# A token's residual row travels with its gathered row, and the scatter writes whole rows (fused graph layer and mixture of experts, one Trainium2 core)

## What is computed

```
xn = layernorm(x)
x  = x + gnn(xn, src, dst, edge_weight) + mix(xn)      # graph sum, linear attention, two small layers
h  = layernorm(x)                                      # "h2" in the kernel
expert = argmax(h @ gate_w + gate_b) ; prb = its softmax value ; pos = rank of the token in its expert
kept   = pos < C                                       # C = ceil(1.25 * 12500 / 8)
y  = (relu(h @ w1[expert] + b1[expert]) @ w2[expert] + b2[expert]) * prb * kept
x  = x + nan_to_num(y, nan=0, posinf=1e4, neginf=-1e4)
```

## Time and profile before

| | |
|---|---|
| three plain runs | 2583.5, 2587.7, 2589.4 us; median 2587.7 us |
| the profiled execution | 2590.2 us, of which the trace spans 2588.4 us |
| PE | 2050 us busy, 79% |
| POOL | 1887 us, 73% |
| PE weight loads | 1593 us, 62% |
| DVE | 1465 us, 57% |
| ACT | 1022 us, 39% |
| DRAM traffic | 503 MB read, 75 MB written, mean 223 GB/s |
| granted TensorE clock, mean | 0.91 of full speed |

### The profile page before, as it was taken

How to read it: one execution, slowest core, us unless ns; L and a number is a source line. 1 busy time by engine, 2 the same in 40 slices (tenths; PEclk the granted TensorE clock), 3 DMA queues, 4 the chain that set the end, 5 groups by cost and what they waited for, 6 DMA issues and landing times. The chain is left out here.

```text
span 2588.4 us, 42537 instructions
## 1 busy us (share of the span) xinstructions
PE 2050.1 (79%) x12806; PEld 1592.5 (62%) x12806; DVE 1464.9 (57%) x5075; ACT 1021.6 (39%) x2450; POOL 1887.3 (73%) x1891
## 2 busy tenths in 40 slices
PE   0079999964677778998889889678888889877687
PEld 0035665543465557777777777557677777676677
DVE  6765555543567777776456456456656656554122
ACT  4643333321444445543343443334443434442233
POOL 7377777777777777777777777777777777736675
PEclk9999999986888889999999999888998989897899
DMA  9755666544566676766776776656887888788997
GB/s 338 258 163 166 174 172 170 167 136 140 171 177 181 176 246 201 220 222 214 229 236 211 231 240 182 214 187 239 297 280 263 268 284 273 262 260 234 295 320 241
DMA packets 294748, 578.36 MB, mean 223 GB/s; under 512 B 51837, under 2 KB 208109, under 8 KB 272271
## 3 DMA queue, kind: packets, MB, share of 16 engines
q1 hardware_dynamic: 164097, 294.27, 33.5%
q0 software_dynamic: 100032, 242.92, 32.7%
q10 hardware_dynamic: 30390, 38.41, 4.1%
HBM read 503.32 MB, written 74.92 MB: 223 GB/s over the span
## 5 line engine op out<-in xcount | busy, mean ns | idle before, releaser
L826 POOL DMA_INDIRECT rows_sb<-xn_scratch,src_sb x1600 | 1549.5, 968 | 526.1 <-issue 519.8
L907 PE MATMUL bank<-rows_sb,s_sb 128*24 128x256 f32 x3200 | 247.9, 433 | 267.3 <-DMA rows_sb<-xn_scratch,src_sb 261.3
L1094 PE MATMUL bank<-acc 128*128 128x256 f32 x1680 | 423.6, 398 | 41.1 <-DVE acc L1583 13.5
L1075 PE MATMUL bank<-acc 128*128 128x128 f32 (+1 forms) x2624 | 437.3, 323 | 15.8 <-issue 15.1
L1075 PEld LDWEIGHTS bank<-acc 128*128 128x128 f32 x2624 | 389.4, 207 | 40.3 <-issue 17.2
L1817 ACT ACTIVATE acc<-bank,acc 128x128 f32<-128x128 f32 (+1 forms) x656 | 212.1, 397 | 452.5 <-PE bank L1075 445.9
L1094 PEld LDWEIGHTS bank<-acc 128*128 128x128 f32 x1680 | 327.2, 202 | 87.2 <-issue 39.5
L1350 DVE TENSOR_TENSOR acc<-acc,bank 128x48 f32 x832 | 170.4, 205 | 293.0 <-PE bank L917 188.9
L907 PEld LDWEIGHTS bank<-rows_sb,s_sb 128*24 128x24 f32 x3200 | 91.5, 110 | 347.9 <-issue 318.9
L1742 ACT COPY sums<-bank 120x256 f32<-120x256 f32 x208 | 76.5, 368 | 395.8 <-PE bank L907 394.2
L1773 ACT ACT_TABLE_LOAD x95 | 121.9, 1283 | 174.7 <-PE bank L996 173.8
(11 more groups left out here) (228 smaller groups left out, 3442.1 us busy)
## 6 DMA issues: line engine op xcount, KB each, us to landing
acc<-ffn_first_in SPq DMA_DIRECT2D x82, 1028.0 KB
acc<-ffn_w_in SPq DMA_DIRECT2D x82, 1024.0 KB
rows_sb<-xn_scratch,src_sb POOLq DMA_INDIRECT x1600
arena<-xn_scratch SPq DMA_DIRECT2D x194, 128.0 KB, 3.1
xnt_scratch<-arena SPq DMA_DIRECT2D x97, 128.0 KB, 2.0
arena<-xnt_scratch SPq DMA_DIRECT2D x97, 128.0 KB
arena<-x_in SPq DMA_DIRECT2D x97, 128.0 KB
h_scratch<-arena ACTq DMA_DIRECT2D x97, 128.0 KB
```

The source lines that it names most:

```text
L826: pool.indirect_dma_start(out=rows_sb[:, c % ROW_SLOTS, :], out_offset=None, in_=xn_d, in_offset=bass.IndirectOffsetOnAxis(ap=src_sb[:, c: ...
L907: m = pe.matmul(psum[0][i * COLS:i * COLS + WIN, 0:D], s_sb[:, p % S_SLOTS, i * GROUP + j, :], early_row(c) if p < EARLY_PAIRS else rows_s ...
L1075: m = pe.matmul(bank[:, i * tokens:(i + 1) * tokens], w1_sb[k % 2][:, h, f * P:(f + 1) * P], xt[:, k % 2, h, 0:tokens], start=h == 0, stop ...
L1094: m = pe.matmul(bank[:, i * D:(i + 1) * D], hid[:, f, i * P:(i + 1) * P], w2_sb[k % 2][:, f, :], start=f == 0 and i == 0, stop=f == FC - 1 ...
```

## The change

- `h2_d` has rows of 2 KB: the layernorm and, behind it, `x` itself. ACT stores both with one DMA (and `out` as before).
- The gather of a unit brings both halves into a ring of eight token tiles, `tok` (2 KB per row). The result is computed in place over the first half, DVE adds the second half to it as the last of its operations, and the scatters, direct and kept, write whole rows without `compute_op`.
- As `tok` is also the place of the result, a gather waits on POOL until the unit that held its tiles before has been stored (`kept_st`) or scattered (`y_st`). DVE's waits for these ahead of L1583 go away.
- DVE cleans tile by tile (the buffers for mask and clipped value are one tile wide).
- The kept units 0 to 20, which SP stored three places behind their last tick's place (`done_place`), are stored one place behind it. All other places stay.

```diff
-    ACC_W = max(WIDE_WINDOWS * WIDE, T * P, N + WIN)
+    ACC_W = max(WIDE_WINDOWS * WIDE, T * P, N + WIN) + 100
+    TOKENS = 8
...
-        h2_d = nc.dram_tensor("h2_scratch", [N, D], F32).ap()
+        h2_d = nc.dram_tensor("h2_scratch", [N, 2 * D], F32).ap()
...
-        xs = behind(1, 2 * UNIT_TILES, D)
+        tok = behind(1, TOKENS, 2 * D)
...
-        yo = behind(1, YS * UNIT_TILES, D)
-        mask_sb = behind(1, UNIT_TILES, D)
-        clip_sb = behind(1, UNIT_TILES, D)
+        mask_sb = behind(1, D)
+        clip_sb = behind(1, D)
...
+        def token_slots(k):
+            at = units[k][1] % TOKENS
+            assert at + size(k) <= TOKENS
+            return slice(at, at + size(k))
+
+        def held_before(k):
+            taken_by = {i for i in range(k) if set(columns_of(i)) & {c - TOKENS for c in columns_of(k)}}
+            return sorted(taken_by)
...
-            lag = 3 if done_place(k) < PAIRS - 3 and size(min(k + 2, K - 1)) == UNIT_TILES else 1
-            scatter_at[min(done_place(k) + lag, PLACES - 1)].append(k)
+            scatter_at[min(done_place(k) + 1, PLACES - 1)].append(k)
...
                 at = col % BACK_ROWS * D
+                if k >= YS:
+                    sp.wait_ge(kept_st[k % YS], kept_value(k - YS))
                 sp.wait_ge(y_done, k + 1)
-                sp.dma_start(kept_d[col // BACK_ROWS, :, at:at + n * D],
-                             yo[:, k % YS * UNIT_TILES:k % YS * UNIT_TILES + n, :].rearrange("p i d -> p (i d)")
-                             ).then_inc(kept_st[k % YS], 16)
+                sp.dma_start(kept_d[col // BACK_ROWS, :, at:at + n * D].rearrange("p (i d) -> p i d", i=n),
+                             tok[:, token_slots(k), 0:D]).then_inc(kept_st[k % YS], 16)
...
                 if k >= 2:
                     pool.wait_ge(x_turned, k - 1)
-                for i, col in enumerate(columns_of(k)):
+                for i in held_before(k):
+                    if i < len(kept):
+                        pool.wait_ge(kept_st[i % YS], kept_value(i))
+                    else:
+                        pool.wait_ge(y_st[i % YS], y_value(i))
+                for col in columns_of(k):
                     pool.indirect_dma_start(
-                        out=xs[:, k % 2 * UNIT_TILES + i, :], out_offset=None, in_=h2_d[0:tokens, :],
+                        out=tok[:, col % TOKENS, :], out_offset=None, in_=h2_d[0:tokens, :],
...
             def scatter_unit(k):
                 tokens = min((routes[batch_of[k]][-1] + 1) * P, N)
+                if k - YS >= len(kept):
+                    pool.wait_ge(y_st[k % YS], y_value(k - YS))
                 pool.wait_ge(y_done, k + 1)
-                for i, col in enumerate(columns_of(k)):
+                for col in columns_of(k):
                     pool.indirect_dma_start(
                         out=out[0:tokens, :], out_offset=bass.IndirectOffsetOnAxis(ap=sca_i[:, col:col + 1], axis=0),
-                        in_=yo[:, k % YS * UNIT_TILES + i, :], in_offset=None, bounds_check=tokens - 1, oob_is_err=False,
-                        compute_op=ALU.add).then_inc(y_st[k % YS], 16)
+                        in_=tok[:, col % TOKENS, 0:D], in_offset=None, bounds_check=tokens - 1, oob_is_err=False
+                    ).then_inc(y_st[k % YS], 16)
...
                     in_=rows_sb[:, s * BACK_ROWS + col % BACK_ROWS, :], in_offset=None,
-                    bounds_check=tokens - 1, oob_is_err=False, compute_op=ALU.add).then_inc(back_st[s], 16)
+                    bounds_check=tokens - 1, oob_is_err=False).then_inc(back_st[s], 16)
...
-                        if k >= YS and k - YS < len(kept):
-                            dve.wait_ge(kept_st[k % YS], kept_value(k - YS))
-                        elif k >= YS:
-                            dve.wait_ge(y_st[k % YS], y_value(k - YS))
...
-                        link(dve.tensor_tensor(mask, y, y, ALU.not_equal))
-                        link(dve.copy_predicated(y, mask, nil[:, :].unsqueeze(2).broadcast_to([P, size(k), D])))
+                        for i in range(size(k)):
+                            link(dve.tensor_tensor(mask, y[:, i, :], y[:, i, :], ALU.not_equal))
+                            link(dve.copy_predicated(y[:, i, :], mask, nil[:, :].broadcast_to([P, D])))
                     elif step == FLUSH:
-                        link(dve.tensor_scalar(clip, y, 10000.0, -10000.0, ALU.min, ALU.max))
-                        link(dve.tensor_scalar(mask, y, 0.0, 0.0, ALU.mult, ALU.not_equal))
-                        dve.copy_predicated(y, mask, clip).then_inc(y_done, 1)
+                        for i in range(size(k)):
+                            link(dve.tensor_scalar(clip, y[:, i, :], 10000.0, -10000.0, ALU.min, ALU.max))
+                            link(dve.tensor_scalar(mask, y[:, i, :], 0.0, 0.0, ALU.mult, ALU.not_equal))
+                            link(dve.copy_predicated(y[:, i, :], mask, clip))
+                        dve.tensor_tensor(y, y, kept_row, ALU.add).then_inc(y_done, 1)
...
-                    act.dma_start(h2_d[t * P:t * P + r, :], c_out[0:r, t % OS, 0, :]).then_inc(c_st[t % OS], 16)
+                    act.dma_start(h2_d[t * P:t * P + r, :], flat2(c_out[0:r, t % OS, :, :])).then_inc(c_st[t % OS], 16)
```

More of the change, by code:

```diff
@@ L252, in build @@
         b2_sb = [behind(1, D) for _ in range(2)]
-        xs = behind(1, 2 * UNIT_TILES, D)
+        tok = behind(1, TOKENS, 2 * D)
         xt = behind(1, 2, H, UNIT)
         hid = behind(1, FC, UNIT)
-        yo = behind(1, YS * UNIT_TILES, D)
-        mask_sb = behind(1, UNIT_TILES, D)
-        clip_sb = behind(1, UNIT_TILES, D)
+        mask_sb = behind(1, D)
+        clip_sb = behind(1, D)
         tab = behind(1, 2 * P)
[L261 to L265, removed]
+        e_wide = behind(0, P)
+        hot_e = behind(0, NE)
+        counted = behind(0, NE)
+        MOST_SLOTS = 20
+        sel = behind(1, 2 * MOST_SLOTS)
+        sprb = behind(0, SLOTS)
         (col_i, col_odd, col_tile, col_from, full_at, one_at, some_at, count, full, fresh, ranked, queue_at, queue_base) = (
-            behind(1, 1) for _ in range(13))
+            behind(0, 1) for _ in range(13))
         ld_gmin, ld_edges, gmin_all = sem("ld_gmin"), sem("ld_edges"), sem("gmin_all")
@@ L607, in build @@
         RANK_AT, SLOT_AT = COUNT_AT + NE, COUNT_AT + NE + 2
+        assert max(tiles_after(b) - tiles_after(b - 1) for b in range(len(routes))) <= MOST_SLOTS
         assert SLOT_AT + 3 * max(tiles_after(b) - tiles_after(b - 1) for b in range(len(routes))) <= 2 * P
@@ L1064, in unit_tick @@
                                 m = pe.transpose(bank[:, (i * H + h) * P:(i * H + h + 1) * P],
-                                                 xs[:, k % 2 * UNIT_TILES + i, h * P:(h + 1) * P], ident[:, :])
+                                                 tok[:, token_slots(k).start + i, h * P:(h + 1) * P], ident[:, :])
                         m.then_inc(x_turned, 1)
@@ L1497, in fill_slots @@
                 token, chance, expert = (psum[6][:, SLOT_AT + i * n:SLOT_AT + (i + 1) * n] for i in range(3))
-                idf, empty = sel[:, 0:n], sel[:, P // 2:P // 2 + n]
+                idf, empty = sel[:, 0:n], sel[:, MOST_SLOTS:MOST_SLOTS + n]
                 link(dve.tensor_copy(expert_i[:, here], expert[0:1, :]))
@@ L1572, in unit_tick @@
                         continue
-                    y = yo[:, k % YS * UNIT_TILES:k % YS * UNIT_TILES + size(k), :]
-                    mask, clip = mask_sb[:, 0:size(k), :].bitcast(I32), clip_sb[:, 0:size(k), :]
+                    y, kept_row = tok[:, token_slots(k), 0:D], tok[:, token_slots(k), D:2 * D]
+                    mask, clip = mask_sb.bitcast(I32), clip_sb
                     if step == 2:
@@ L1822, in unit_tick @@
                         for i, col in enumerate(columns_of(k)):
-                            y = yo[:, k % YS * UNIT_TILES + i, :]
+                            y = tok[:, col % TOKENS, 0:D]
                             act.activation(y, y, ACT.Copy, scale=sprb[:, col:col + 1]).then_inc(y_scaled, 1)
```

## The result

The kernel after took 2572.4 us in the median of four runs (2569.2 to 2581.3), beside 2588.5 for the kernel before on the same chip: a ratio of 0.9948, 95% interval 0.9931 to 0.9965. So it is faster by 0.2 to 0.5%, 6 to 16 us, and the forecast of 2566 erred on the hopeful side. The profiled execution is the slowest of the four, 2581.3 us with a span of 2579.6; it stands against 2590.2 and 2588.4.

What follows compares the result with a forecast made beforehand. The DMA engines were taken to bound the last 326 us, POOL's edge gathers the stage before. Terms -22 - 3 + 3 + 0.4 - 0.6 = -22 us from 2590.2 give 2568, 2566 by the median; own range 2555 to 2578.

Steps and rivals of the forecast that it cites:

- The adds in the tail: After the last edge gather: plain scatters save 30.6 us of DMA time; POOL's shorter scatters -3, less full engines +3.
- the 22 of the sum: Whole kernel: all terms together -22 us; scatters less 2 KB gathers in the tail alone gave -22.
- The second KB: Tail: gathering 2 KB rows adds 8 to 11 us of DMA time, 8.6 taken; POOL and edge stage 0.
- rival D: 79 gathers before 2262 us: a 2 KB row costs POOL two descriptors each way, 76 us; time 2641; chance 0.07.
- DVE (0): Edge stage: 1.5 us more per two-tile unit, 23 units, hidden, so 0; 34 us if the cover were gone.
- POOL's new wait: Edge stage: a unit's gather waits for the store of the unit eight columns before; +0, at most some 5 us.
- rival E: Edge stage: POOL stands at the new wait in all 17 two-tile gathers, 3 us each, 51 us; chance 0.05 with unseen.
- The edges' gathers: POOL up to 2262 us: they run without a gap and still end near 2262 us; change 0.
- SP's waits are only what decides who is late: Tail: the DMA engines, 102% busy, are the bound; SP's 61.3 us of waits decide who is late.
- rival B: Tail: SP's waits are the real bound; PE's 37 us of weight waits go; -45 us, about 2544; chance 0.22.
- The lead of POOL: Edge stage: POOL's six places of lead take up most of any late rows on PE; 0 us.

Runs made afterwards that it cites:

- plain_before: The kernel before with the add taken from both scatters and nothing else: 2551.4 us, ratio 0.9867 to the kernel before.
- store_first: The kernel after with the store ahead of `load_second` in SP's place: 2556.4 us, ratio 0.9882 to the kernel before.
- second session: The kernel after, unchanged, measured again: 2579.9 us, ratio 0.9977 to the kernel before.
- store_ahead: store_first with kept groups 5 to 9 loaded into free memory, so SP does not wait for a slot's scatters: 2544.8 us, ratio 0.9841 to the kernel before.
- before_ahead: The kernel before with kept groups 5 to 9 loaded into free memory, on the slower chip: ratio 0.9964 to the kernel before.
- add_back: The kernel after with the add back in both scatters and without DVE's add, on the slower chip: ratio 1.0286 to the kernel before.
- add_back_2: The kernel after with the add back in both scatters and without DVE's add of the residual: 2614.1 us, ratio 1.0104 to the kernel before.

## Why the prediction was right, and where it was not

- **The adds in the tail (-30.6 of DMA time, -3, +3).** Right, and the largest term. plain_before shows -30.0 us of tail, 3.2 us per MB for a plain scatter where I took 3.5, and 1.02 us on POOL where I took 0.97. In the kernel after the period is 8.94 us; 8.8 was predicted. The tail of the kernel after is 19 us shorter in one execution and 26 in the other, around the 22 of the sum.
- **The second KB (+8.6 in the tail, nothing on POOL, nothing in the edge stage).** Right in kind, a little too dear: 6 us. POOL's cost per gather did not move, which ends rival D. That agrees with what the prediction drew from the Trainium skill ("DMA: Bandwidth & Descriptors", SWDGE vs HWDGE vs iDMA), a cost by rows and not by bytes. The share in the edge stage went to 45.4 + 33.0 + 5.0 = 83% between 1900 and 2200 us, under the 86 expected, and POOL's wait for PE from 6.0 to 8.1 us.
- **DVE (0).** Right: 1465 to 1526 us busy, and neither POOL nor the edges' stage shows it.
- **POOL's new wait (+0, at most 5).** This step failed: it is 24 to 25 us. The mechanism was named, also as rival E, whose 51 us were right in the place and double in the size: six gathers of 17 wait, 4 us each in the mean. The working gave the store 0.5 us of issue behind DVE's last operation, and named as the condition that it is issued at once. It then looked only at what the store stands ahead of, the node loads, and not at what stands ahead of the store: `load_second` in the same place. The row that would have said so was in the trace of the kernel before. Its waits of SP between 1080 and 1580 us:

```profile
SPq L707 <- DVE acc L1583: 106.2, 18, 18.7
```

  Eighteen times in 500 us SP stands at the line just ahead of the store, 6 us in the mean and once 19. With the order mended the working is sound: in store_first the tightest gather (unit 15's) comes 8.1 us behind the start of DVE's last operation, the store goes out 0.8 us behind it, and the gather does not wait.
- **The edges' gathers (0).** Not foreseen: -8 to -13 us of POOL's time in the two profiles of the kernel after (1541.9 and 1537.0 for 1549.5), from a line that nobody edited. It hides a third to a half of the failed step. That the total fell near the forecast is luck in part: two errors of opposite sign met. In the second session the kernel took 2579.9, a little above the 2555 to 2578 that the forecast gave as its own range.
- **"SP's waits are only what decides who is late" against rival B.** Half right. B's 45 us did not come: behind 2372 us SP's waits for scatters fell from 61.3 to 37.7 us only, and PE's waits for weights from 37 to 23. But taking SP's waits away is worth 11 us both with the adds gone (store_ahead, at a DMA share of 0.96 for 0.97) and with them (before_ahead, on the slower chip). The share near 1 was not proof that the engines could carry no more: they moved 312 GB/s at 1.03, 351 at 0.95, and 378 at 0.96. Single slices of 4.5 us reach 431 in store_ahead, so the ceiling of 435 that the prediction cites from the Trainium skill ("DMA: Bandwidth & Descriptors", Where 436 GB/s comes from) fits these runs, and the mean stays under it.
- **The lead of POOL.** The text ahead of the prediction says that the ring of edge rows holds 48 tiles, up to six places. It holds 24 (`ROW_SLOTS` is 6 x `LOAD`, and `LOAD` is 4), which at 8 tiles per place is three places. The prediction leant on six places only as cover for late rows, and no wait of PE came of it.

By terms, in us of the whole time: the adds -34 (30 foreseen; this holds the faster gathers too), the second KB and DVE +6 (8 foreseen), POOL's wait +24 (0 foreseen). That is -4; measured are -16 in the first session and -6 in the second.

## What to carry to other kernels

When a wait is moved to an engine on the critical path, read the stream of the engine that releases it, line by line: what counts is not how early the data is ready but which waits stand ahead of the releasing instruction in its queue. Here the exchange of two lines in SP's place was worth 24 us, more than the whole change. An add inside an indirect DMA is dear where DMA engines or POOL are short: carry the old value along in the gather, and let an engine with time add it.

## What the runs showed of the hardware

- A plain indirect scatter of 128 rows of 1 KB takes POOL 1.0 us, one that adds 1.57, a gather 0.97 to 0.98 whether its rows have 1 or 2 KB. On the DMA engines the plain scatter costs about 3.2 us per MB and the adding one 7.3.
- If indirect DMAs of the program add, POOL's gathers are longer, also those many hundred us before the first that adds: the shortest edge gather between 700 and 1000 us takes 947 to 950 ns with (five profiles) and 940 to 942 without (nine). In the mean it is 3 to 8 ns, 6 to 10 on the slower chip, so 5 to 16 us over 1600 gathers. Why it is so no run tells.
- The busy share of the DMA engines says little about their room: at 0.95 to 1.03 they moved between 312 and 378 GB/s, by what the packets were (312 is with the adds) and, it seems, by how steadily they were asked for; that last part is argued and not shown.
- One of the chips runs the same kernel 21% slower, with its own kind of wait, and there POOL's wait for the stores was three times as long (77 for 24.6 us, add_back and add_back_2, the same kernel). A margin of a few us that holds on one chip need not hold on the next.
